# Two-layer macaron kernel on one core: order of clearing, weight transfers and token statistics in the expert assignment

## What is computed

```python
def _L0_ffn_ref(x, gate_w, gate_b, w1, b1, w2, b2):
    E, K, C = 64, 3, 128
    xf = x.reshape(-1, D)                      # x is layernormed before
    logits = xf @ gate_w + gate_b
    top_l, top_i = jax.lax.top_k(logits, K)
    gates = jax.nn.softmax(top_l, axis=-1)
    oh = jax.nn.one_hot(top_i.reshape(-1), E, dtype=jnp.int32)
    pos = (jnp.cumsum(oh, axis=0) * oh).sum(-1) - 1
    valid = pos < C
    ...                                        # gather rows, two matmuls with a gelu between, scatter back
x = x + 0.5 * _L0_ffn_ref(_layernorm(x), ...)
```

## Time and profile before

| | us |
|---|---|
| median of the runs (3) | 3161.79 |
| lowest, highest | 3155.25, 3163.49 |
| the profiled execution, its device time | 3150.57 |
| the profiled execution, its span | 3148.8 |
| PE busy in the span | 2839.0 (90%) |
| DMA busy, mean over the span; the queue of SP | 45.5% |

### The profile page before, as it was taken

One profiled execution on the slowest core, in us unless ns is written; L12 is line 12 of the kernel. 1 busy time (PEld: TensorE's weight loads), 2 busy tenths in 40 slices (PEclk: granted clock), 3 DMA queues, 4 the chain that ended last, 5 costly groups with the idle time before them and its releaser, 6 DMA issues. The chain is left out here.

```text
span 3148.8 us, 54094 instructions
## 1 busy us (share of the span) xinstructions
PE 2839.0 (90%) x19481; PEld 2042.4 (65%) x19481; DVE 1666.4 (53%) x4549; ACT 1539.0 (49%) x2605; POOL 1306.5 (41%) x1303
## 2 busy tenths in 40 slices
PE   4899999758889988678999997999879999989999
PEld 3799999733344443358999996666546666655666
DVE  4411111178888888463111111666676666655666
ACT  1133333239999998311333332333257777772333
POOL 3544444349998889254444442000044444320000
PEclk9899999979999999868999998999989999998999
DMA  8199999711655555752999996000152344201000
GB/s 284 41 306 327 329 327 325 234 30 18 64 63 62 62 63 62 96 198 86 328 327 326 327 326 203 1 0 0 32 124 72 87 96 101 72 1 38 13 13 20
DMA packets 359857, 431.97 MB, mean 137 GB/s; under 512 B 86193, under 2 KB 314566, under 8 KB 356550
## 3 DMA queue, kind: packets, MB, share of 16 engines
q1 hardware_dynamic: 335046, 395.30, 45.5%
q0 software_dynamic: 24576, 33.57, 5.0%
HBM read 355.93 MB, written 72.88 MB: 136 GB/s over the span
## 5 line engine op out<-in xcount | busy, mean ns | idle before, releaser
L1675 ACT ACTIVATE f_h_t<-f_h_ps,f_b_t 128x128 f32<-128x128 f32 x1024 | 320.2, 364 | 596.3 <-PE f_h_ps L1633 596.3
L2062 POOL TENSOR_TENSOR a_dmg_buf<-a_c 128x2048 f32<-128x2048 f32 x128 | 520.1, 4091 | 85.2 <-DVE a_c L2544 42.7
L1633 PEld LDWEIGHTS f_h_ps<-f_rows_t,f_w 128*128 128x128 f32 x4096 | 481.4, 193 | 9.9 <-issue 3.5
L1633 PE MATMUL f_h_ps<-f_rows_t,f_w 128*128 128x128 f32 x4096 | 482.6, 276 | 2.3 <-DVE f_rows_t L1687 1.2
L1647 PE MATMUL f_y_ps<-f_w,f_h_t 128*128 128x256 f32 x2048 | 483.4, 379 | 0.0
L1593 POOL DMA_INDIRECT acc_rows<-f_y,f_give x128 | 205.1, 1603 | 487.2 <-DMA acc_rows<-f_y,f_give 451.6
L1647 PEld LDWEIGHTS f_y_ps<-f_w,f_h_t 128*128 128x128 f32 x2048 | 369.8, 190 | 39.9
L1687 DVE COPY f_rows_t<-f_t_ps 128x256 f32<-128x256 f32 x128 | 54.4, 425 | 598.4 <-PE f_t_ps L1621 593.7
L2411 DVE SCALAR_TENSOR_TENSOR a_bond_buf<-a_a,a_small_rep,a_q_ps 128x512 f32<-128x512 f32 x512 | 346.8, 740 | 5.3 <-PE a_q_ps L2238 2.2
L428 DVE SCALAR_TENSOR_TENSOR x_resid<-f_y_ps,f_gate,x_resid 128x256 f32 x512 | 218.8, 479 | 161.1 <-PE f_y_ps L311 155.5
L885 ACT ACTIVATE a_prob<-a_prob,a_neg_top 128x384 f32<-128x384 f32 (+3 forms) x512 | 276.5, 569 | 47.9 <-POOL a_neg_top L702 47.7
(11 more groups left out here) (337 smaller groups left out, 4110.4 us busy)
## 6 DMA issues: line engine op xcount, KB each, us to landing
f_w<-in_L_ffn_w_dram SPq DMA_DIRECT2D x256, 1024.0 KB
a_skewed<-skew SPq DMA_DIRECT2D x32, 512.0 KB, 7.2
a_k_s<-parts SPq DMA_DIRECT2D x16, 768.0 KB, 7.9
acc_rows<-x_resid SPq DMA_DIRECT2D x17, 512.0 KB, 5.3
xn_rows<-f_xn SPq DMA_DIRECT2D x16, 512.0 KB, 3.0
x_resid<-acc_rows SPq DMA_DIRECT2D x16, 512.0 KB, 8.3
a_vals<-val_rows SPq DMA_DIRECT2D x64, 128.0 KB, 4.2
skew<-a_bond SPq DMA_DIRECT2D x128, 64.0 KB
```

Of the source, the lines that this page charges most:

```text
L1633: last = nc.tensor.matmul(h_ps[n // HB][:, (n % HB) * P:(n % HB + 1) * P], w1_sb[s][:, c, n * P:(n + 1) * P], rows_t[e % 2][:, c, :], star ...
L1675: nc.scalar.activation(h_t[k][:, n, :], h_ps[n // HB][:, (n % HB) * P:(n % HB + 1) * P], ACT.Gelu, bias=b1_t[:, n, e:e + 1]).then_inc(gelu ...
L2062: nc.gpsimd.tensor_tensor(dmg_buf[n % RING][:, :, :], places(c_sb[h], first_place(dg)), c_sb[h][:, PAD:].unsqueeze(1).broadcast_to([P, DG, ...
```

## The change

- `load_phase` clears only the spare rows of `acc_rows`. `skew` and `val_rows` are cleared in the first `route`: `skew` behind batch 4's stores, `val_rows` behind batch 5's. The second `route` clears nothing.
- In both routes the weights of expert i (i below 4) are issued behind the stores of batch i, and `b1_rows` behind those of batch 4. They were ahead of all batches.
- The statistics of batches 2 to 7 are split into batches 2 and 3, which stay where they were, and batches 4 to 7, which DVE takes between `mark(0)` and `weigh(0)`. Their root comes on ACT between `exps(0)` and `copy_base(1)`, their inverse on DVE behind `weigh(0)`. POOL's `normalise(i)` waits only for its own group.
- ACT's order for the first three roots stays the same, only written out.

```diff
--- before.py
+++ after.py
@@ -57,6 +57,12 @@
                 self.x_loaded[i], 16)
         self.x_loads += 1
 
+    def clear(self, sp, rows):
+        view = rows.rearrange("(n p r) d -> n p r d", p=P, r=TPB)
+        for m in range(rows.shape[0] // (P * TPB)):
+            sp.dma_start(view[m], self.x[:, (B + 1) * TPB:, :]).then_inc(self.cleared, 16)
+            self.clears += 1
+
     def wait_x(self, eng, i):
         eng.wait_ge(self.x_loaded[i], 16 * self.x_loads)
 
@@ -68,7 +74,7 @@
         return self.x[:, n * TPB + j, :]
 
 
-def load_phase(core, x_dram, scratch):
+def load_phase(core, x_dram, spare_rows):
 
 
     nc = core.nc
@@ -81,12 +87,7 @@
         def _(sp):
             core.load_x(sp, x_dram.rearrange("b s d -> (b s) d"))
             sp.wait_ge(spare_zeroed, 1)
-            per = TPB
-            for rows in scratch:
-                view = rows.rearrange("(n p r) d -> n p r d", p=P, r=per)
-                for m in range(rows.shape[0] // (P * per)):
-                    sp.dma_start(view[m], core.x[:, (B + 1) * TPB:, :]).then_inc(core.cleared, 16)
-                    core.clears += 1
+            core.clear(sp, spare_rows)
 
         @block.gpsimd
         def _(pool):
@@ -1106,7 +1107,7 @@
         return rows[i * S:(i + 1) * S, :].rearrange("(j p) d -> p j d", p=P)
 
 
-def ffn0_phase(core, sparse, name, gate_w, gate_b, w1, b1, w2, b2):
+def ffn0_phase(core, sparse, name, to_clear, gate_w, gate_b, w1, b1, w2, b2):
     nc = core.nc
     E, H = w1.shape[0], w1.shape[2]
     HC = H // P
@@ -1134,13 +1135,13 @@
             sp.dma_start(b2_row[s][:, :], b2[e:e + 1, :]).then_inc(w_loaded[s], 16)
 
         route(core, sparse, name, gate_w, gate_b, E, b1, b1_rows, b1_loaded, take, give, gate, xn_stored, acc_stored,
-              load_weights, R)
+              load_weights, R, to_clear)
         experts(core, sparse, name, E, H, R, b1_rows, b1_loaded, w1_sb, w2_sb, b2_row, take, give, gate, acc_stored,
                 w_loaded, load_weights)
 
 
 def route(core, sparse, name, gate_w, gate_b, E, b1, b1_rows, b1_loaded, take, give, gate, xn_stored, acc_stored,
-              load_weights, R):
+              load_weights, R, to_clear):
 
 
 
@@ -1220,7 +1221,7 @@
         table_done = sem("r_table")
         block = ctx.enter_context(nc.Block())
 
-        ROOTS = ((0, 1), (1, 2), (2, B))
+        ROOTS = ((0, 1), (1, 2), (2, 4), (4, B))
 
         def wait_xn(eng, i):
 
@@ -1233,14 +1234,18 @@
         def _(sp):
             sp.dma_start(gate_w_sb[:, :, :], gate_w.rearrange("(c p) e -> p c e", p=P)).then_inc(w_loaded, 16)
             sp.dma_start(gate_b_sb[:, :], gate_b.partition_broadcast(3)).then_inc(b_loaded, 16)
-            for s in range(R):
-                load_weights(sp, s, s)
-            sp.dma_start(b1_rows[:, :], b1).then_inc(b1_loaded, 16)
             for i in range(B):
                 core.wait_x(sp, i)
                 sp.dma_start(sparse.batch(sparse.acc, i), core.x_batch(i)).then_inc(acc_stored, 16)
                 wait_xn(sp, i)
                 sp.dma_start(sparse.batch(sparse.xn, i), xn[i % 2][:, :, :]).then_inc(xn_stored[i % 2], 16)
+
+                if i < R:
+                    load_weights(sp, i, i)
+                if i == R:
+                    sp.dma_start(b1_rows[:, :], b1).then_inc(b1_loaded, 16)
+                if 0 <= i - R < len(to_clear):
+                    core.clear(sp, to_clear[i - R])
             for k in range(2):
                 sp.wait_ge(xn_stored[k], 16 * (B // 2))
 
@@ -1263,7 +1268,7 @@
 
             def normalise(i):
                 k = i % 2
-                pool.wait_ge(rstd_ready, 2 if i == 1 else len(ROOTS))
+                pool.wait_ge(rstd_ready, 1 + [a <= i < b for a, b in ROOTS].index(True))
                 if i >= 2:
                     pool.wait_ge(xn_stored[k], 16 * (i // 2))
                     pool.wait_ge(turned, DC * (i - 1))
@@ -1394,13 +1399,20 @@
                 act.wait_ge(counted, i)
                 nc.scalar.copy(base_row[:, :], count_ps[0:1, 0:E]).then_inc(base_ready, 1)
 
-            for n, (a, b) in enumerate(ROOTS):
+            def root(n):
+                a, b = ROOTS[n]
                 act.wait_ge(var_ready, n + 1)
                 nc.scalar.activation(std[:, a * TPB:b * TPB], std[:, a * TPB:b * TPB], ACT.Sqrt).then_inc(std_ready, 1)
-                if n < 2:
-                    copy_turned(n)
+
+            root(0)
+            copy_turned(0)
+            root(1)
+            copy_turned(1)
+            root(2)
             for i in range(B):
                 exps(i)
+                if i == 0:
+                    root(3)
                 if i + 1 < B:
                     copy_base(i + 1)
                 if i + 2 < B:
@@ -1520,14 +1532,18 @@
             inverse_std(1)
             dve.wait_ge(consts, 2)
             nc.vector.tensor_copy(before[:, :], before_f[:, :]).then_inc(before_ready, 1)
-            statistics(2, B)
+            statistics(2, 4)
             inverse_std(2)
             for i in range(B):
                 choose(i)
                 mark(i)
                 if i:
                     locate(i - 1)
+                else:
+                    statistics(4, B)
                 weigh(i)
+                if i == 0:
+                    inverse_std(3)
             locate(B - 1)
             read_table()
 
@@ -2697,12 +2713,13 @@
         skew = nc.dram_tensor("skew", (P, TPB * (D // 16) * 2 * WIN), FP32, kind="Internal").ap()
         val_rows = nc.dram_tensor("val_rows", (2 * S, D), FP32, kind="Internal").ap()
         parts = nc.dram_tensor("parts", (2, DC, 6, P, S), BF16, kind="Internal").ap()
-        load_phase(core, t["L0_attn_x"], (sparse.acc[B * S:, :], skew.rearrange("p (r d) -> (p r) d", d=D), val_rows))
+        load_phase(core, t["L0_attn_x"], sparse.acc[B * S:, :])
+        to_clear = [skew.rearrange("p (r d) -> (p r) d", d=D), val_rows]
         order = phases.split()
         for n, ph in enumerate(order):
             core.free_semaphores()
             if ph == "f0":
-                ffn0_phase(core, sparse, f"f0_{n}", *[t["L0_ffn_" + s] for s in
+                ffn0_phase(core, sparse, f"f0_{n}", to_clear if n == 0 else [], *[t["L0_ffn_" + s] for s in
                            ("gate_w", "gate_b", "w1", "b1", "w2", "b2")])
             if ph == "f1":
                 ffn1_phase(core, f"f1_{n}", *[t["L1_ffn_" + s] for s in
```

## The result

| | before | after |
|---|---|---|
| median of the runs, us | 3162.64 (4 runs) | 3130.72 (4 runs) |
| lowest, highest | 3155.25, 3169.56 | 3124.23, 3134.84 |
| span of the profiled execution | 3148.8 | 3133.1 |

The change makes the kernel 31.9 us faster, ratio 0.989 with a 95% interval of 0.987 to 0.991. The interval of the ratio reaches from 28 to 40 us. The forecast was a gain of 32.7 us and a time of 3129.1; that it came within 2 us of the measured time is closer than this measurement can tell.

A forecast was written before the change was run, and what follows sets the result against it. PE, busy for 90% of the span, was taken as the bound, so starting places(1) earlier saves time at the end. Gains of 21.5 + 11.2 = 32.7 us off the median 3161.79 gave 3129.1, range 3115 to 3142.

The forecast's parts named there:

- What POOL waited for: In both routes, POOL's normalise(2) waits for batch 0's xn store, issued behind all the weights; waits 20.2 and 17.92 us.
- First route, 21.5 us at places(1): In the first route, PE's places(1) start at 42.5 instead of 64.03, 21.5 us earlier.
- the barrier 3.4 us earlier: End of load_phase: six fewer issues on SP, so the barrier opens 3.4 us earlier.
- the 8.1 of the sum: First route: gate_b lands at 16.6, so split_bias, normalise(1), turn(1) and logits(1) start 8.1 us earlier.
- Second route, 11.2 us: In the second route, PE's places(1) start at 1371.3 instead of 1382.53, 11.2 us earlier.
- The stretch from places(1) to the last table unchanged: PE is the bound there in each route; the first route's 75.6 us, with one wait of 1.17 us, stays.
- Statistics behind the first choice at nothing: DVE's 6.7 us of statistics behind choose(0) and mark(0) are hidden by 3.2 us of slack on xn(3).
- Two table loads more per route: ACT loads Sqrt and Exp again, 1.28 us each, costed at nothing; at most 2.6 us per route.
- Stores behind weights: On SP, no batch's store waits behind more than the previous batch's weight set, issued a round before; cost nothing.
- First rival: PE's clock rises before places(1), shortening a round from 16.4 to 9.7 us, twice: 13.4 more, 3115.7; chance 0.12.
- Second, third and fourth rival: First-route gate_b late, 3137.2, 0.14; PE clock stays 1.2 GHz, 3189, 0.04; store not POOL's wait, 3158.4, 0.03.
- The sum: Both routes' gains at places(1), 21.5 + 11.2 = 32.7 us, taken from the median 3161.79: 3129.1.

The follow-up runs named there:

- e4: The changed kernel with the weights of the first four experts and b1_rows ahead of all batches again; 3163.3 us, ratio to before 0.998.
- e2: The kernel before with only the split of statistics and roots, clearing and weights as before; 3169.3 us, ratio to before 1.000.
- e3: The changed kernel with the clearing of skew and val_rows back in the load phase; 3138.3 us, ratio to before 0.990.
- e1: The changed kernel with one group of statistics for batches 2 to 7 again, transfers in the new order; 3142.2 us, ratio to before 0.991.
- e9: e8's later statistics and 18, 18, 16 added matmuls around turn(0) and logits(0), plus 5 before each later round's logits; 3109.6 us, ratio to before 0.980.
- e7: The changed kernel with statistics of batches 4 to 7 behind weigh(1), their root behind copy_turned(3); 3137.7 us, ratio to before 0.991.
- e11: e9 with the statistics of batches 4 to 7 behind mark(0), as in the change; 3116.6 us, ratio to before 0.984.
- e8: e7 plus unread PE matmuls: 18 before and 18 behind turn(0), 16 behind logits(0), 5 behind turn(1) to turn(3); 3116.0 us, ratio to before 0.984.
- e10: e9 with 12 instead of 5 added matmuls before each later round's logits; 3127.4 us, ratio to before 0.986.

## Why the prediction was right

- **What POOL waited for** (the landing of batch 0's store, called "issue" by the profile): right. e4 brings the wait back with only the weights, e2 shows that the split without the transfers does nothing, and in both the wait ends within 0.2 us of the store's landing.
- **First route, 21.5 us at places(1)**: measured 64.03 - 42.41 = 21.6. Its terms: the barrier 3.4 us earlier (SP's first issue of the route at 9.96 instead of 13.31); `gate_b` used at 16.72, worked out 16.6; normalise(2) at 26.61, worked out near 27. e3 takes this part away again: 7.2 us at places(1), near the 8.1 of the sum.
- **Second route, 11.2 us**: 43.4 - 31.7 = 11.7. Of the 0.5 us more, 0.3 are there at logits(0) already (8.0 us into the route instead of 8.3); I did not follow their cause.
- **The stretch from places(1) to the last table unchanged**: 75.0 us against 75.6, and in the second route 75.9 against 75.1. That it held rests partly on chance: over the two routes of e1 to e4 the same stretch took 72.5 to 78.7 us, as its tables fell to the low clock more or less often. Of e3's and e4's misses of 5 and 6 us, 2.5 and 3.9 come from there. The prediction also counts one wait in it; PE has five more of 0.7 to 0.8 us in before, for ACT's copies, and these are the gaps that e9 fills.
- **Statistics behind the first choice at nothing**: right at the end, but with less slack than worked out. normalise(3) ran 7.02 us where the sum had 4.9, a size that was too small though the place was right, so xn(3) was ready at 45.2, 1.1 us before PE wanted it at 46.3, not 3.2. e7 shows that still nothing came through, and e11 what it costs once the slack is gone.
- **Two table loads more per route**: there (ACT has 8 in the two routes instead of 4, 1.28 us each) and hidden; ACT waited 7.03 us for the statistics behind the first of them.
- **Stores behind weights**: xn stores of the first route landed 2.9 to 5.8 us after their issue, where the first took 10.6; none held POOL.
- **First rival**: it did not come, at a chance of 0.12. The Trainium skill (TensorE: Matmul & The Clock Gate, section on why this matters for your kernels) advises work without gaps. The trace agrees only in part: PE had no gap above 0.7 us from 26 to 54 us and stayed low, and e8 fell with a gap of 0.21 us at most; but with the gaps filled by added matmuls, e9 was high from turn(0) on in both routes, but for turn(3) and the added matmuls behind it in the first. The rival's price of 13.4 us, for the round behind places(1) in both routes, was too high: in e9 that round takes 13.9 and 12.3 us where the change has 16.4 and 15.6, 5.8 us in sum, since POOL's xn(3) is the next limit. e9 gains more than this, its routes end 11.9 and 12.0 us before the change's, because places(1) come earlier (3.5 and 2.5 us) and the later rounds are shorter (5.9 and 6.2 us); neither was in the rival.
- **Second, third and fourth rival**: `gate_b` came early; the clock rose in the first table, or within three matmuls of its end, in both routes of every kernel without added matmuls; the wait was the store. The prediction says that this table ended high in both routes of before. In the first one it did not: the table took 5.49 us, low from end to end, and the clock rose in the places behind it (0.72 us).
- **The sum**: 32.7 forecast, 31.9 measured, with an interval of 28 to 40. Both routes came out 0.1 and 0.5 us from their terms at places(1); the agreement of the whole times is luck beyond that, since other stretches of the program move by more.

## What to carry to other kernels

When a double-buffered loop stands before a wait that the profile can't name, look for what is queued in front of the store that frees the buffer: here 8 MB of weights that nobody wanted for 100 us were ahead of the half MB store for whose landing POOL, and behind it PE, stood waiting. Ask of each transfer when it is first used, and issue it behind what is used earlier; one part of such a change can be worth little or nothing without the other (e2, e4). And when PE is the bound, read the duration of one repeated group over time: if it jumps between two values, filling PE's waits with added matmuls may be worth trying before the next reordering (e9 is 21 us under the change by the medians, 29 by the ratio), as long as they fit into the waits (e9 against e10). Then look again at what had been hidden (e11).

## What the runs showed that was not expected

- A group of 24 table matmuls takes 2.94 us at one clock level and 5.49 at the other, and the rounds of a kernel fall and rise in an order that differs from route to route. Two versions that reach places(1) 7 us apart (e3 and the change) ended only 4.7 apart. The same instructions with the same waits, within 0.01 us, just before them ran low in one place and high in another: the count of round 0 in e8 and e9 (0.80 and 0.51 us), turn(3) in e9's two routes (1.97 and 1.09).
- POOL's normalise of one batch takes 4.83 us beside an idle DVE, 4.88 beside `bn_stats`, 5.05 beside choose, mark and `bn_stats`, and 6.9 to 7.0 us beside choose, mark and locate. It is the same in the two routes of the change (7.02, 7.01 us) and of e3 (7.01, 7.02). The trace of before had the hint: its normalise in later rounds took 5.8 to 6.0 us.
- The first attention varies by 20 us between executions with the same code (719 to 742 us), where the forecast missed the measured gain by 0.8. A single profiled execution hid half of a gain of 1% here; the stretches that a change touches agree far better (139.6 and 139.3, 118.5 and 118.5).
